# Five blocks of tiles (2, 2, 4, 4, 4) instead of four of 4 in a fused decoder layer

## What is computed

```python
# 1 state space layer, as a convolution by FFT, and its own norm
y = irfft(rfft(x, 2048) * rfft(K, 2048))[:1024]
x = layernorm(x + (norm(x + y + x * D) * ln_w + ln_b))
# 2 attention over the context, 16 heads of 16
attn = softmax((x @ Wq.T + bq) @ (ctx @ Wk.T + bk).T / 4)
x = layernorm(x + (attn @ (ctx @ Wv.T + bv)) @ Wo.T + bo)
# 3 feed-forward: a gated MLP and an expert layer with product keys
sim = einsum(x @ Wq2, keys)              # 2 x 4 heads x 64 keys
scores, idx = top 8 of 8 x 8 sums of the top 8 of each half
w = silu(x . down_embed[idx]) * softmax(scores)
x = layernorm(x + silu(x @ Wg + bg) * (x @ Wu + bu) @ Wd + bd + sum(w * up_embed[idx]))
```

## Time and profile before

| | us |
|---|---|
| median of 3 runs (lowest, highest) | 707.53 (706.36, 708.19) |
| profiled execution, span | 700.8 |
| PE busy | 590.3 (84%) |
| DVE busy | 506.6 (72%) |
| ACT busy | 404.9 (58%) |
| POOL busy | 279.9 (40%) |

### The profile page before, as it was taken

The page is one execution under the profiler, slowest core; times in us unless marked ns, Lnnn a source line. Parts: engine busy times, 40 slices in busy tenths (PEclk is TensorE's granted clock), DMA queues, the critical chain, the costliest instruction groups (busy, mean ns, idle before and its releaser), DMA issues.

```text
span 700.8 us, 9712 instructions
## 1 busy us (share of the span) xinstructions
PE 590.3 (84%) x3132; PEld 383.4 (55%) x3132; DVE 506.6 (72%) x1046; ACT 404.9 (58%) x593; POOL 279.9 (40%) x333
## 2 busy tenths in 40 slices
PE   5743587785296778999999999999999999899996
PEld 2512366563264554445678565478575479453485
DVE  7999985523047885898866879767778797578783
ACT  4971655222042435797763878675579765577760
POOL 0002871635041345543343634235635234644361
PEclk9876989898596567999999999999999999999999
DMA  8945030456325000000000000000000000000000
GB/s 239 363 204 91 1 98 2 119 162 144 89 83 217 1 1 1 0 1 0 1 1 0 17 8 7 1 1 1 9 8 8 8 1 1 8 16 7 0 8 23
DMA packets 20111, 34.27 MB, mean 49 GB/s; under 512 B 7388, under 2 KB 14045, under 8 KB 18333
## 3 DMA queue, kind: packets, MB, share of 16 engines
q1 hardware_dynamic: 15677, 29.46, 13.7%
q10 hardware_dynamic: 4384, 4.20, 2.0%
HBM read 21.94 MB, written 10.65 MB: 47 GB/s over the span
## 4 chain that ended last, share of the span: by engine, by line
PE 60%; DVE 22%; ACT 7%; issue 6%; POOL 3%; DMA 1%; SPq 0%; ACTq 0%; DVEq 0%; POOLq 0%
PE banks L773 20%; PE banks L863 8%; PE banks L868 7%; PE banks L818 4%; PE banks L840 3%; PE banks L795 3%; PE banks L830 3%; PE banks L804 2%; PE banks L715 2%; DVE stats L1377 2%; ACT arena L882 2%; PE banks L651 2%; DVE arena L1468 2%; PE banks L855 2%; ACT arena L1067 1%
## 5 line engine op out<-in xcount | busy, mean ns | idle before, releaser
L1169 POOL TENSOR_TENSOR arena<-arena 128x1024 f32<-128x1024 f32 x64 | 125.8, 1965 | 156.6 <-ACT arena L1067 155.6
L773 PE MATMUL banks<-arena 128*128 128x512 f32 x384 | 174.6, 596 | 5.4 <-issue 3.7
L773 PEld LDWEIGHTS banks<-arena 128*128 128x128 f32 x384 | 69.9, 190 | 83.2 <-issue 76.5
L1067 ACT ACTIVATE arena<-arena 128x1024 f32<-128x1024 f32 x64 | 73.5, 1149 | 7.5 <-DVE arena L1466 3.2
L1069 ACT ACTIVATE arena<-arena 128x1024 f32<-128x1024 f32 x64 | 73.5, 1149 | 2.1
L1468 DVE SCALAR_TENSOR_TENSOR arena<-arena 128x1024 f32<-128x1024 f32 x48 | 63.8, 1329 | 1.7
L863 PE MATMUL banks<-arena 128*128 128x256 f32 x256 | 58.4, 381 | 2.4 <-DVE tok L1504 1.2
L957 ACT COPY arena<-banks 128x512 f32<-128x512 f32 (+1 forms) x64 | 34.1, 532 | 44.8 <-PE banks L765 29.3
L868 PE MATMUL banks<-arena 128*128 128x256 f32 x256 | 57.9, 379 | 0.0
L1142 POOL TENSOR_SCALAR arena<-mv 128x1 f32<-128x1 f32 (+1 forms) x40 | 14.1, 353 | 105.2 <-DVE mv L1378 103.8
L971 ACT ACTIVATE tok<-tok,arena,rstd 128x256 f32<-128x256 f32 x48 | 27.9, 598 | 45.5 <-POOL arena L1147 44.6
(11 more groups left out here) (179 smaller groups left out, 1077.4 us busy)
## 6 DMA issues: line engine op xcount, KB each, us to landing
scr_x<-arena SPq DMA_DIRECT2D x16, 256.0 KB, 3.2
arena<-scr_x SPq DMA_DIRECT2D x2, 2048.0 KB, 13.8
arena<-scr_z SPq DMA_DIRECT2D x32, 128.0 KB
scr_z<-arena ACTq DMA_DIRECT2D x14, 256.0 KB, 7.1
tok<-in_x SPq DMA_DIRECT2D x8, 256.0 KB, 5.7
out<-tok SPq DMA_DIRECT2D x16, 128.0 KB, 1.7
arena<-in_imat SPq DMA_DIRECT2D x1, 1152.0 KB, 5.6
arena<-in_fmat SPq DMA_DIRECT2D x1, 1088.0 KB, 7.0
```

The lines of the kernel that those rows point to most:

```text
L773: ins = mm(bk[:, :], w[:, k, P * m:P * m + P], src[:, k, :], start=(k == 0), stop=(k == KC - 1))
L1067: fn(ebuf[m % 2], sxb[m % 2], ACT.Prelu, bias=negt[:, n % 2, h:h + 1], alpha=FAR).then_inc(s_ranked, 1)
L1169: tt(sxb[m % 2], sim[:, n % 2, h, 0:XR].unsqueeze(2).broadcast_to((P, XR, NKEYS)), sim[:, n % 2, FH + h, :].unsqueeze(1).broadcast_to((P, ...
```

## The change

Blocks get the sizes 2, 2, 4, 4, 4 (`BLOCKS`). Two tables give the due step of each tile's attention (`ATTEND_AT`) and feed-forward (`FEED_AT`). Attention of tiles 0 to 3 stays at steps 0 to 3; tiles 4 to 7 are due half a step apart, at 4, 4.5, 5 and 5.5 (their places inside the step are scaled by `pace`); tiles 8 to 15 are due at steps 6 to 13 instead of 8 to 15. Feed-forward of tile n is due at step n + 2 instead of n + 4. For a block of two, `expert`, `inner` and `query` have 256 columns, all 8 `expert` and 4 `inner` are due in its first step, and the other 4 `inner`, the spreads and the first `outer` in its second. The buffers `hid` of the two small blocks take only the first half of the space, so that tiles 8 to 15 of `rconv` stay free of them, and the four `ln` / `residual` groups of tiles 8 to 15 move from 1.94, 2.37, 3.03 and 3.14 to 2.3, 3.2, 4.1 and 4.9. All other lines replace `SUPER * n` by the block's first tile and 512 columns by the block's own.

```diff
--- before.py
+++ after.py
@@ -47,6 +47,11 @@
 NF = D // 2
 
 
+BLOCKS = ((0, 2), (2, 2), (4, 4), (8, 4), (12, 4))
+ATTEND_AT = (0, 1, 2, 3, 4, 4.5, 5, 5.5, 6, 7, 8, 9, 10, 11, 12, 13)
+FEED_AT = (2, 3, 4, 5, 6, 7, 8, 9, 10, 11, 12, 13, 14, 15, 16, 17)
+
+
 N1, N2 = 2 * NC, NFFT // (2 * NC)
 PAIRS = [(0, NC)] + [(2 * m - 1, 2 * m) for m in range(1, FREQ - 1)] + [(NC - 1,)]
 
@@ -57,7 +62,7 @@
          "pair": (0.283, 0.3896, 0.7908, 0.8005), "total": (0.847,), "first": (-0.1,), "sums": (-0.805,),
          "exps": (-0.131,), "late": (-0.027, 0.0075, 0.6998),
          "conv": (-2.338, -1.7122, -1.4984, -1.4216, -1.3318, -1.294, -1.1762, -0.9644),
-         "ln": (-1.672, -1.4042, 0.3146, 1.2224, 1.9378, 2.3695, 3.0308, 3.1386),
+         "ln": (-1.672, -1.4042, 0.3146, 1.2224, 2.3, 3.2, 4.1, 4.9),
          "ln_steps": (-0.336, -0.234, 0.162, 0.013, 0.361), "sines": (-3.002, -2.884), "tables": (0.0,),
          "taps": (0.982,), "x_second": (-0.756, 0.69), "skip": (0.382,), "k_first": (5.96, 0.01, 9.6, 0.059),
          "simw": (-1.866,), "x_bias": (2.891, 0.086), "values": (2.518,), "diagonal": (-1.627,),
@@ -101,19 +106,26 @@
     return chunk * P // NKV, min((chunk * P + P - 1) // NKV, HEADS - 1)
 
 
+def block_of(tl):
+
+    s = max(s for s, (first, _) in enumerate(BLOCKS) if first <= tl)
+    return s, tl - BLOCKS[s][0]
+
+
 def plan():
 
 
     steps = []
 
-    def put(start, kind, n, *rest, key=None, j=0):
-        steps.append((start + PLACE[key or kind][j], (kind, n) + rest))
+    def put(start, kind, n, *rest, key=None, j=0, pace=1.0):
+        steps.append((start + pace * PLACE[key or kind][j], (kind, n) + rest))
         return steps[-1][0]
 
-    def queries(start, s):
-        for kind in ("turn1", "query"):
-            for j in range(2):
-                put(start, kind, s, j, j=j)
+    def queries(start, s, pace=1.0):
+        for j in range(BLOCKS[s][1] // 2):
+            put(start, "turn1", s, j, j=j, pace=pace)
+        for j in range(2):
+            put(start, "query", s, j, j=j, pace=pace)
 
     def normed(at, tl, k):
         put(at, f"dev{k}", tl)
@@ -121,7 +133,11 @@
 
     def products(f, i):
 
-        r = SUPER * f
+        r, size = BLOCKS[f]
+        if size == 2:
+            if i == 0:
+                return [("expert", f, c) for c in range(FC)] + [("inner", f, c) for c in range(4)]
+            return [("inner", f, c) for c in range(4, 8)] + [("spread", r, 0), ("spread", r, 1), ("outer", r)]
         if i == 0:
             return [("expert", f, c) for c in range(6)]
         if i == 1:
@@ -141,30 +157,32 @@
     for h in range(2):
         put(-1, "score", 0, h, j=h)
     for tl in range(TILES):
-        s, i = divmod(tl, SUPER)
-
-        start = tl
-        alone = "_alone" if tl < SUPER - 1 else ""
+        s, i = block_of(tl)
+        size = BLOCKS[s][1]
+
+        start = ATTEND_AT[tl]
+        pace = ATTEND_AT[tl + 1] - start if tl + 1 < TILES else 1.0
+        alone = "_alone" if tl == 0 else ""
         for j in range(3):
-            put(start, "probs", tl, j, key="probs" + alone, j=j)
-        put(start, "attend", tl, key="attend" + alone)
-        put(start, "turno", tl, key="turno" + alone)
-        normed(put(start, "project", tl, key="project_last" if i == SUPER - 1 else "project" + alone), tl, 2)
-        if i == SUPER - 1 and s + 1 < NSUP:
-            queries(start, s + 1)
+            put(start, "probs", tl, j, key="probs" + alone, j=j, pace=pace)
+        put(start, "attend", tl, key="attend" + alone, pace=pace)
+        put(start, "turno", tl, key="turno" + alone, pace=pace)
+        normed(put(start, "project", tl, key="project_last" if i == size - 1 else "project" + alone, pace=pace), tl, 2)
+        if i == size - 1 and s + 1 < len(BLOCKS):
+            queries(start, s + 1, pace)
         if tl + 1 < TILES:
             for h in range(2):
-                put(start, "score", tl + 1, h, key="score" + alone, j=h)
-
-        start = tl + SUPER
+                put(start, "score", tl + 1, h, key="score" + alone, j=h, pace=pace)
+
+        start = FEED_AT[tl]
         if i == 0:
-            for j in range(2):
-                put(start, "turn2", s, j, j=j)
-            put(start, "sim", tl, key="sim_first")
+            for j in range(size // 2):
+                put(start, "turn2", s, j, j=j + 2 - size // 2)
+            put(start + (0.04 if size == 2 else 0.0), "sim", tl, key="sim_first")
             put(start, "best", tl, key="best_first")
         work = products(s, i)
         for k, y in enumerate(work):
-            lo, hi = PLACE["products"][2 * i:2 * i + 2]
+            lo, hi = PLACE["products"][2 * i:2 * i + 2] if size == SUPER else (0.04 - 0.04 * i, 1.0 - 0.03 * i)
             at = start + lo + (hi - lo) * (k + 0.5) / len(work)
             steps.append((at, y))
             if y[0] == "outer":
@@ -177,7 +195,7 @@
                               (kind, tl, h)))
         put(start, "first", tl)
         put(start, "total", tl)
-        if i < SUPER - 1:
+        if i < size - 1:
             put(start, "sim", tl + 1)
             put(start, "best", tl + 1)
         else:
...
@@ -374,6 +392,7 @@
         o_w = o_wt + 10240
         silg = part("silg", o_w, EC, W)
         hid = part("hid", o_w + 4096, FC, W)
+        hid_of = [hid if size == SUPER else part(f"hid{s}", o_w + 4096, FC, P * size) for s, (_, size) in enumerate(BLOCKS)]
         rconv = part("rconv", o_w + 4096, TILES, D)
         x2T = part("x2T", o_w + 8192, KC, W)
         sim = part("sim", o_w + 9216, 2, 2 * FH, NKEYS)
@@ -763,14 +782,14 @@
...
             def wide(key, w, m, src):
 
-                bk = w_unit(key)
+                bk, n = w_unit(key), P * BLOCKS[key[1]][1]
                 for k in range(KC):
-                    ins = mm(bk[:, :], w[:, k, P * m:P * m + P], src[:, k, :], start=(k == 0), stop=(k == KC - 1))
+                    ins = mm(bk[:, 0:n], w[:, k, P * m:P * m + P], src[:, k, 0:n], start=(k == 0), stop=(k == KC - 1))
...
@@ -1476,22 +1495,23 @@
                     own.done(s_rr)
                 elif kind == "expert":
                     th = tanh_at(step)
-                    stt(silg[:, step[2], :], th, 1.0, w_bank(W_AT[step + ("a",)])[:, :], ALU.add,
+                    w = P * BLOCKS[n][1]
+                    stt(silg[:, step[2], 0:w], th, 1.0, w_bank(W_AT[step + ("a",)])[:, 0:w], ALU.add,
                         ALU.mult).then_inc(s_wdve, 1)
...
```

More of the change, by code:

```diff
@@ L844, in _ @@
                         pe.wait_ge(s_ffn_in, 16 * 5)
-                        pe.wait_ge(s_tev, T_AT[("turn2", n, 1)] + 1)
+                        pe.wait_ge(s_tev, T_AT[("turn2", n, BLOCKS[n][1] // 2 - 1)] + 1)
                     wide(step + ("a",), dn, step[2], x2T)
@@ L858, in _ @@
                 elif kind == "outer":
-                    i = n % SUPER
-                    pe.wait_ge(s_wdve, max(DVE_TURN[("inner", n // SUPER, c, "A")] for c in range(FC)))
+                    f, i = block_of(n)
+                    pe.wait_ge(s_wdve, max(DVE_TURN[("inner", f, c, "A")] for c in range(FC)))
                     bk = w_unit(step + ("o",))
                     for c in range(FC):
-                        mm(bk[:, 0:D], hid[:, c, P * i:P * i + P], wd[:, c, :], start=(c == 0), stop=False)
+                        mm(bk[:, 0:D], hid_of[f][:, c, P * i:P * i + P], wd[:, c, :], start=(c == 0), stop=False)
                     pe.wait_ge(s_wdve, DVE_TURN[("spread", n, 1, "d")])
@@ L966, in wide_ready @@
                 act.wait_ge(*W_DONE[u])
-                return w_bank(u)[:, :]
+                return w_bank(u)[:, 0:P * BLOCKS[key[1]][1]] if key[0] in ("query", "expert", "inner") else w_bank(u)[:, :]
             def normalise(k, tl, s_done, last=True):
@@ L1028, in _ @@
                     if n:
-                        act.wait_ge(*W_DONE[max(W_AT[("inner", n - 1, FC - 1, "A")], W_AT[("sim", SUPER * n - 1, "a")])])
+                        act.wait_ge(*W_DONE[max(W_AT[("inner", n - 1, FC - 1, "A")], W_AT[("sim", BLOCKS[n][0] - 1, "a")])])
                     turned_tokens(step, step[2], x2T)
@@ L1160, in _ @@
                     for i in range(2):
-                        tl = SUPER * n + 2 * step[2] + i
+                        tl = BLOCKS[n][0] + 2 * step[2] + i
                         tt(tok[:, tl, :], tok[:, tl, :], bias, ALU.add).then_inc(s_added, 1)
@@ L1493, in _ @@
                 elif kind == "spread":
-                    j, i, u = step[2], n % SUPER, W_AT[step + ("d",)]
+                    j, i, u = step[2], block_of(n)[1], W_AT[step + ("d",)]
                     dve.wait_ge(*W_DONE[u])
```

32 lines of the change are left out of this document (16 added, 16 removed).

## The result

The changed kernel takes 773.78 us (median of 4 runs, 769.21 to 777.03) against 707.86 us of the kernel before (4 runs, 706.36 to 716.37): a ratio of 1.096, 95% interval 1.087 to 1.105. It is slower, as forecast, but by 66 us and not by 22; the range ended at 741.

The account below looks back on a forecast made before the run. PE set the pace before; DVE and list order were to bound the changed stage. Waits at full length gave 158.7 us from 252.0, +27, taken as 22: span 722.8 plus 6.7 around it, 729.5 us; range 705 to 741.

Parts of the forecast that it names:

- The start: Up to `best` of tile 0: forecast at 252.0 us, 29.2 us earlier than in the kernel before.
- PE's work: `sim` of tile 0 to `project` of tile 7: about 118 us of PE without idle, 2 us for half clock.
- rival C: Whole kernel: waits at full length and clock halved in PE's pauses, +27 and up to 10 more, above 741; chance 0.08.
- DVE's work: `best` of tile 0 to `project` of tile 7: 121.3 us, more than PE's; break-even needs 92% of 131.7 us.
- (a): From `best` of tile 0: PE stands about 8 us at `expert` 5, DVE then waits; 31.4 us of work in 38.8.
- (b): Step 3: 25.8 us of DVE work in 32.1, ending with tile 3's norm between its `project` and `turn2`.
- (c): POOL's `dev1` of tiles 12, 13 before `sums` of tile 2 delays ACT: 7.7 us in all, 21.3 in 29.0.
- (d): PE has `outer` of tile 1 just ahead of `project` of tile 4; DVE waits 8.3 us for `project`.
- (e): On to `project` of tile 7: 42.8 us each of DVE and PE, interleaved with waits for each other, take 50.5.
- 85% gave 11: `best` of tile 0 to `project` of tile 7: at the earlier kernel's 85% DVE share, 142.7 us, so +11.
- A: Whole kernel faster: DVE packs as in one step at 90% busy, list orders bite little; 697.1 us; chance 0.12.
- B: Whole kernel slower by little: DVE bounds, only forced waits count; +5, 712.4 us; chance 0.21.

Follow-up runs that it names:

- re-timed kernel: The changed kernel, same blocks and instructions, with all due times chosen anew: 702.52 us, ratio 0.994 to the kernel before.
- filled run: The changed kernel with 193 idle matmuls ahead of PE's twelve longest waits: 754.30 us, ratio 1.075 to the kernel before.
- run with the early norms: The changed kernel with the norms of tiles 8 to 15 back at their old places: 754.41 us, ratio 1.068 to the kernel before.
- swapped orders: The changed kernel with `sums` of tile 2 before `dev1` on POOL, `project` of tile 4 before `outer` of tile 1 on PE: 757.47 us.
- four-orders run: The changed kernel with old norm places, two step pairs swapped, and in blocks of 2 second `best` later, `exps` earlier: 749.54 us, ratio 1.062.

## Why the prediction was right and wrong

**The direction and the place: right.** What the change costs lies before `project` of tile 7; 318.5 us behind it against 317 forecast. The start, `best` of tile 0 at 255.1, is 3.1 us late, and the first transposition was 4.1 us late already. From the end of `project` of tile 1 on PE to this `best` it is 10.0 us, as forecast; in the working, 242.0, 3.2 and 1.6 make 246.8 and not 247.4, and the 0.73 us that PE waits ahead of `sim` are about what is missing. The 6.7 us added around the span are mis-sized in their reading, not in the total: 1.8 lie around a span, and the rest is that the profiled execution was a quick one.

**PE's work: nearly right at full clock, and that was the condition.** 118 us forecast from `sim` of tile 0; 124.7 with the pauses filled, 154.3 as the kernel ran. "Full clock from there" was named as a sign, and the clock was 0.80. The working allowed 2 us for half clock, "at the first products", and rival C had "up to 10 more" at a chance of 0.08. It measures 20 us of path in this kernel. The view for it was read: in the earlier trace rows attention alone has a clock of 0.69 where PE pauses. The step from there to a stage with some 40 us of forecast pauses (158.7 less 118) that will not keep its clock was not made.

**DVE's work: the sum was right (121.3 us forecast; 111.9 and 280 gaps of 0.03 are 120.3), its reading was wrong.** "DVE above 80% busy from 252" did not come: 60%. DVE doesn't bound this stage; the re-timed kernel packs 103.8 us of such work at 92%. The 85% of the kernel before was taken as what an in-order list reaches. In the kernel before PE was busy 104 of 105.8 us over that stage, so there it may as well be what DVE was asked for; no run tells the two apart.

**The waits: the places right, the sizes wrong. This is the step that failed.** They were found by laying the due times side by side, at the right places and with the right releasers. The lengths worked out for them, 158.7 us in all, were too short by 43:

| | forecast | measured | |
|---|---|---|---|
| (a) `best` of tile 0 to the end of step 2 | 38.8 | 44.9 | PE stood 9.71 at `expert` 5 for 8 forecast |
| (b) to `best` of tile 2 | 32.1 | 40.5 | |
| (c) to the end of DVE's work ahead of (d) | 29.0 | 33.8 | DVE's waits 13.1 for 7.7; PE stood 9.92 at `attend` of tile 4 |
| (d) `project` of tile 4 | 8.3 | 12.06 | `outer` and `project` at full clock, 7.9; 4.0 of other products ahead of them, in part at half clock |
| (e) to `project` of tile 7 | 50.5 | 70.4 | |
| sum | 158.7 | 201.6 | |

Each term is too low, (e) by the most, 19.9 us. Two things were left out or sized too small, and a third was taken off.

First, the clock: 20 us over the five, by the filled run. In (e), 56.5 us of PE for 42.8 forecast.

Second, ACT's and POOL's lists. The wait (c) on POOL was found:

```profile
349.26 0.25 POOL L1161 TENSOR_SCALAR arena<-mv 128x2 f32<-128x2 f32 x1 [11.86 <-DVE mv L1397]
...
350.94 5.86 POOL L1188 TENSOR_TENSOR arena<-arena 128x1024 f32<-128x1024 f32 x3
```

Others were not, or were priced too low. In (a), four `exps` and a norm stand ahead of the tanh of `inner` 0 (timeline of ACT):

```profile
284.94 0.38 ACT L1005 ACTIVATE arena<-banks 128x256 f32<-128x256 f32 x1 [6.79 <-PE banks L792]
285.35 1.15 ACT L1086 ACTIVATE arena<-arena 128x1024 f32<-128x1024 f32 x1
286.53 1.15 ACT L1088 ACTIVATE arena<-arena 128x1024 f32<-128x1024 f32 x1
287.71 1.15 ACT L1086 ACTIVATE arena<-arena 128x1024 f32<-128x1024 f32 x1
288.90 1.15 ACT L1088 ACTIVATE arena<-arena 128x1024 f32<-128x1024 f32 x1
290.08 1.09 ACT L990 ACTIVATE tok<-tok,arena,rstd 128x256 f32<-128x256 f32 x2
291.20 0.47 ACT L1066 ACTIVATE arena<-banks,pcol 128x256 f32<-128x256 f32 x1
```

ACT had waited while PE stood, and it waited 6.79 us more while PE worked off `attend` and a `score` at half clock from 277.20 on. When the next product came, all that had gathered was ahead of the one tanh that frees PE's bank, and PE stood again, 3.85 us, at 292.09. The prediction had 3.5 us of DVE's time for these `exps` and the first `inner` together; DVE waited 6.30 us for this tanh. In (e) PE and DVE wait for a tanh again, behind a norm that ACT gets late from POOL (timelines of POOL, then ACT):

```profile
410.04 0.39 POOL L1161 TENSOR_SCALAR arena<-mv 128x2 f32<-128x2 f32 x1 [21.04 <-DVE mv L1397]
...
411.87 1.90 POOL L1188 TENSOR_TENSOR arena<-arena 128x1024 f32<-128x1024 f32 x1
415.74 1.90 POOL L1188 TENSOR_TENSOR arena<-arena 128x1024 f32<-128x1024 f32 x1 [1.97 <-ACT arena L1086]
417.74 0.25 POOL L1161 TENSOR_SCALAR arena<-mv 128x1 f32<-128x1 f32 x1
...
420.56 0.19 POOL L1166 TENSOR_TENSOR arena<-arena,rstd 128x1 f32<-128x1 f32 x1
```

```profile
420.85 1.73 ACT L990 ACTIVATE tok<-tok,arena,rstd 128x256 f32<-128x256 f32 x3 [4.09 <-POOL arena L1166]
422.60 0.72 ACT L1028 ACTIVATE arena<-arena 128x616 f32<-128x616 f32 x1
```

Behind it comes the tanh at 423.72 that ends PE's wait of 4.51 us at 424.24 and DVE's of 7.85. It looks like the wait (c) once more, made by the last norm pair at 4.9: its `dev1` waits 21.04 us for DVE and holds POOL's list. The run with the early norms says otherwise. There this `dev1` isn't in the way, and the wait is still there, 3.33 us on PE and 6.67 on DVE (timelines of POOL, ACT, PE):

```profile
394.17 1.91 POOL L1188 TENSOR_TENSOR arena<-arena 128x1024 f32<-128x1024 f32 x1 [2.54 <-ACT arena L1086]
```

```profile
399.21 0.60 ACT L990 ACTIVATE tok<-tok,arena,rstd 128x256 f32<-128x256 f32 x1 [4.03 <-POOL arena L1166]
```

```profile
401.48 2.07 PE L792 MATMUL banks<-arena 128*128 128x256 f32 x4 [3.33 <-ACT arena L1005]
```

The chain is `exps` on ACT, the second `sums` behind it on POOL, the two `dev2` behind that, their norm on ACT and then the tanh. The late pair adds only about 1.2 us to it, its two `norm1` that ACT does in the same place (1.73 us for 0.60). The prediction priced no such chain in (e).

Third, the trim: "some will overlap, and 85% gave 11. I take 22." The full sum was +27, and it was trimmed toward a figure that rested on DVE's share. That is 5 us of the 44 by which the forecast was short; untrimmed it would have stood at 734.5. The waits came out longer than their full sum instead of overlapping: while PE stands, ACT and DVE run out of work and then have it in a heap. How the 43 us over the 158.7 divide: 20 to the clock, by the filled run; the other 23, by difference, to the lists. The re-timed run shows that all of it goes with other due times, but apart from (c) and (d), which the swapped orders take away, into which waits it goes is read from the timelines and not shown run by run. The four-orders run speaks against adding such waits up as if each could be had alone.

**The rivals.** A (faster) was wrong for this kernel, but its price, 697.1, is near what the same blocks give with other due times, 702.5: the blocks of 2 come within 5 us of what its sum said, and the due times of the change don't reach it. B (only the forced waits, 712) was too low. C is the one that came: the waits at full length and half clock in PE's pauses, "above 741". Its own sum, +27 and up to 10 more, ends at 744.5, 29 us short, since the waits grew beyond their full length too.

## What to carry to other kernels

Where engines work through fixed lists, as here, the sum of each engine's work said what the change may reach, and the order of the lists what it did: 702.5 and 773.8 us for the same instructions. When the waits that a new order makes are found by hand, don't trim their sum for overlap; look for every list that has the same pattern, ACT's and POOL's too, and look for products at half clock behind each pause of PE of some microseconds, and add them. A restructured stage wants its due times chosen anew before it is judged.

## What the runs showed of the hardware

Idle matmuls buy time. With 193 products that compute nothing, the granted clock between `best` of tile 0 and `project` of tile 7 rose from 0.80 to 0.98 and the kernel got 19 us faster by the medians; half as many gave 9. In the attention-alone stretch of the kernel before 52 of them raised the clock from 0.69 to 0.91 and no gain could be told (0.994 to 1.002): a higher clock by itself bought nothing there. The clock has two levels, 1.2 and 2.4 GHz, in the durations too: 8 records of 256 columns in 3.78 or 1.89 us. In the changed kernel it stood at the lower after waits of 9.71, 5.10 and 4.51 us, and after one of 2.24 us too (8 records in 3.59 us at 405.13); in the re-timed kernel a wait of 1.15 us was followed by 8 records in 1.99 us. The Trainium skill, TensorE: Matmul & The Clock Gate, section HAM oscillation — how this bites in real kernels, describes a matmul kernel that pays for its waits with half clock again and again; the trace agrees, with waits for other engines in the place of its waits for DMA.
